# Contraction of the stacked attentions' score products: 96 rows before, 128 rows after, with 32 rows of zeros

## What is computed

```
q = _split_heads(x_q @ wq.T + bq)
k = _split_heads(x_kv @ wk.T + bk)
v = _split_heads(x_kv @ wv.T + bv)
scores = jnp.einsum('bhqd,bhkd->bhqk', q, k) * scale
attn = jax.nn.softmax(scores, axis=-1)
out = jnp.einsum('bhqk,bhkd->bhqd', attn, v)
return out @ wo.T + bo
...
x = x + _L1_xattn_ref(_layernorm(x, axis=-1), ctx_1024, ...)
x = x + _L1_ffn_ref(_layernorm(x, axis=-1), ...)
```

## Time and profile before

| | us |
|---|---|
| median of 3 runs | 4145.89 |
| lowest, highest | 4144.44, 4151.56 |
| the profiled execution, its own time | 4147.24 |
| span of the profiled execution, first to last instruction | 4145.4 |
| PE busy in the span | 3406.9 (82%) |
| DVE busy | 3363.0 (81%) |
| ACT busy | 2312.2 (56%) |
| POOL busy | 1555.2 (38%) |

### The profile page before, as it was taken

How to read it: one execution, slowest core, us unless ns; L and a number is a source line. 1 busy time by engine, 2 the same in 40 slices (tenths; PEclk the granted TensorE clock), 3 DMA queues, 4 the chain that set the end, 5 groups by cost and what they waited for, 6 DMA issues and landing times. The chain is left out here.

```text
span 4145.4 us, 95469 instructions
## 1 busy us (share of the span) xinstructions
PE 3406.9 (82%) x31830; PEld 2483.1 (60%) x31831; DVE 3363.0 (81%) x6145; ACT 2312.2 (56%) x4244; POOL 1555.2 (38%) x907
## 2 busy tenths in 40 slices
PE   6983979998599799994038839999499998899999
PEld 3553647776477477763026627777366666677777
DVE  7888879998799799996025569999788888788888
ACT  2431657776277466661025527777566665466665
POOL 1210035653000355542754435555155553122222
PEclk9985989999599899995569969999699998899999
DMA  1001222222000222211111242222222222000000
GB/s 64 14 27 68 124 52 64 67 63 54 36 0 0 53 63 63 63 40 46 52 53 59 63 123 67 61 64 61 60 58 51 52 57 75 26 16 15 13 12 15
DMA packets 158968, 208.77 MB, mean 50 GB/s; under 512 B 37820, under 2 KB 109824, under 8 KB 155585
## 3 DMA queue, kind: packets, MB, share of 16 engines
q1 hardware_dynamic: 149441, 187.83, 16.6%
q0 software_dynamic: 8192, 16.92, 1.2%
q10 hardware_dynamic: 1152, 1.57, 0.2%
HBM read 53.09 MB, written 42.21 MB: 23 GB/s over the span
## 5 line engine op out<-in xcount | busy, mean ns | idle before, releaser
L727 ACT ACTIVATE a_p<-a_p 128x480 f32<-128x480 f32 x832 | 503.2, 605 | 449.9 <-DVE a_p L572 442.8
L354 POOL TENSOR_TENSOR a_km<-a_k,a_slots 96x1920 fp32r<-96x1920 f32 x186 | 629.3, 3402 | 179.0 <-DMA a_k<-a_kh 179.0
L567 DVE TENSOR_REDUCE a_mx<-a_sc 128x4 f32<-128x480 f32 (+1 forms) x832 | 540.5, 650 | 67.2 <-PE a_sc L821 43.7
L572 DVE TENSOR_TENSOR a_p<-a_sc,a_mx 128x480 f32<-128x480 f32 x832 | 532.3, 640 | 19.1 <-issue 0.3
L733 ACT ACTIVATE a_pt<-a_tp 120x512 f32<-120x512 f32 x832 | 486.1, 585 | 77.0 <-PE a_tp L830 72.9
L830 PE MATMUL a_tp<-ident,a_p 128*120 128x128 f32 x3328 | 507.6, 275 | 4.1 <-ACT a_pt L733 4.1
L830 PEld LDWEIGHTS a_tp<-ident,a_p 128*120 128x120 f32 x3328 | 404.6, 138 | 80.0 <-issue 29.7
L815 PE MATMUL a_sc<-a_km,a_qr 96*128 96x480 f32 x768 | 396.9, 517 | 41.7 <-DVE a_p L572 24.6
L854 PE MATMUL a_nd<-a_pt,a_vm 120*32 120x128 f32 x6656 | 289.9, 281 | 9.4 <-ACT a_pt L733 9.0
L1806 ACT ACTIVATE f_s<-f_pu 128x512 f32<-128x512 f32 x256 | 153.7, 600 | 212.4 <-PE f_pv L1288 212.4
L854 PE MATMUL a_nd<-a_pt,a_dm 120*32 120x128 f32 x6656 | 263.7, 273 | 0.0
(11 more groups left out here) (431 smaller groups left out, 8853.2 us busy)
## 6 DMA issues: line engine op xcount, KB each, us to landing
a_qr<-a_qh SPq DMA_DIRECT2D x372, 64.0 KB, 2.0
a_k<-a_kh SPq DMA_DIRECT2D x384, 60.0 KB, 2.0
a_ctx<-in_ctxT SPq DMA_DIRECT2D x64, 240.0 KB, 2.7
a_qr<-a_ql SPq DMA_DIRECT2D x186, 64.0 KB, 2.0
a_k<-a_kl SPq DMA_DIRECT2D x192, 60.0 KB, 2.0
dispatched<-f_empty SPq DMA_DIRECT2D x8, 1040.0 KB, 21.0
f_xr<-dispatched SPq DMA_DIRECT2D x32, 260.0 KB, 2.6
chosen<-f_none SPq DMA_DIRECT2D x8, 1024.0 KB, 11.9
```

Of the source, the lines that this page charges most:

```text
L354: v.tensor_tensor(KM[par][:, i, :, :].rearrange("p b (j k) -> p b j k", k=KN), K3[:, i, :, :].unsqueeze(2).to_broadcast([TR, GB, 4, KN]), ...
L567: v.tensor_reduce(mx[:], view, AX.X, ALU.max).then_inc(mx_ready, 1)
L572: v.tensor_tensor(PR[s % 4][:].rearrange("p (h k) -> p h k", k=k), view, mx[:].unsqueeze(2).to_broadcast([P, heads, k]), ALU.subtract).the ...
L727: a.activation(PR[s % 4][:], PR[s % 4][:], ACT.Exp).then_inc(exp_ready, 1)
```

## The change

The tensors K3, QR and KM get 128 rows in place of 96, and `slots` too. Rows 96 to 127 are zeroed once per phase. The DMAs still fill rows 0 to 95. `masked_keys` now runs over 128 rows, so KM's last 32 rows become zero times zero, and L815 contracts over 128 rows; its number of columns stays. On DVE, four memsets per stacked phase are new: K3's, `slots`' and the first QR's rows behind `ln_group(0)`, the second QR's behind `masked_keys` of the opening. Two semaphores tell of them: POOL waits for the first before its first `masked_keys`, PE for the second before the first step and before every odd group.

```
-            K3 = sb(n_("k3"), [TR, 4, GB, KN])
-            QR = [sb(n_(f"qr{i}"), [TR, 4, GT], F32R) for i in range(2)]
+            K3 = sb(n_("k3"), [P, 4, GB, KN])
+            QR = [sb(n_(f"qr{i}"), [P, 4, GT], F32R) for i in range(2)]
...
-        slots = sb(n_("slots"), [TR, 4] if packed else [P, 4, STRIDE])
-        KM = [sb(n_(f"km{i}"), [TR, 4, GB, W], F32R) if packed else ...
+        slots = sb(n_("slots"), [P, 4] if packed else [P, 4, STRIDE])
+        KM = [sb(n_(f"km{i}"), [P, 4, GB, W], F32R) if packed else ...
...
                 low_part("k", 0)
+                pool.wait_ge(keys_empty, 2)
                 masked_keys(pool, nc.gpsimd, 0, 0, (0, 2))
...
                 ln_group(0)
+                if packed:
+                    v.memset(K3[TR:P], 0.0).then_inc(keys_empty, 1)
+                    v.memset(slots[TR:P], 0.0).then_inc(keys_empty, 1)
+                    v.memset(QR[0][TR:P].bitcast(F32), 0.0).then_inc(queries_empty, 1)
                 if bo is not None:
...
                 if packed:
                     dve.wait_ge(keys_first_in, 16 * n_first)
+                    dve.wait_ge(keys_empty, 2)
                     masked_keys(dve, v, 0, 0, (1, 3))
+                    v.memset(QR[1][TR:P].bitcast(F32), 0.0).then_inc(queries_empty, 1)
                 groups_loop(dve, group, 3 if U == 1 else 1)
...
                     if packed and j == 0:
+                        if i == 0 and par == 1:
+                            pe.wait_ge(queries_empty, 2)
                         pe.wait_ge(km_ready[i], g + 1)
...
+                if packed:
+                    pe.wait_ge(queries_empty, 1)
                 if own_keys:
                     groups_in_full(group)
```

More of the change, by code:

```diff
@@ L278, in attention_phase @@
             LOW = {"k": sb(n_("kl"), [P, GB * KN], F32R), "q": sb(n_("ql"), [P, GT], F32R)}
-            K3 = sb(n_("k3"), [TR, 4, GB, KN])
-            QR = [sb(n_(f"qr{i}"), [TR, 4, GT], F32R) for i in range(2)]
+            K3 = sb(n_("k3"), [P, 4, GB, KN])
+            QR = [sb(n_(f"qr{i}"), [P, 4, GT], F32R) for i in range(2)]
         CTX = [sb(n_(f"ctx{i}"), [P, GB, KN]) for i in range(2)] if not own_keys else None
-        slots = sb(n_("slots"), [TR, 4] if packed else [P, 4, STRIDE])
-        KM = [sb(n_(f"km{i}"), [TR, 4, GB, W], F32R) if packed else sb(n_(f"km{i}"), [P, GB, U, W]) for i in range(2)]
+        slots = sb(n_("slots"), [P, 4] if packed else [P, 4, STRIDE])
+        KM = [sb(n_(f"km{i}"), [P, 4, GB, W], F32R) if packed else sb(n_(f"km{i}"), [P, GB, U, W]) for i in range(2)]
         VW = D if hepos else NH * 32
@@ L316, in attention_phase @@
         prep_pool = sem(n_("prep_pool"))
+        keys_empty, queries_empty = sem(n_("keys_empty")), sem(n_("queries_empty"))
         f_psum = sem(n_("f_psum"))
@@ L354, in masked_keys @@
                 v.tensor_tensor(KM[par][:, i, :, :].rearrange("p b (j k) -> p b j k", k=KN),
-                                K3[:, i, :, :].unsqueeze(2).to_broadcast([TR, GB, 4, KN]),
-                                slots[:].unsqueeze(1).unsqueeze(3).to_broadcast([TR, GB, 4, KN]),
+                                K3[:, i, :, :].unsqueeze(2).to_broadcast([P, GB, 4, KN]),
+                                slots[:].unsqueeze(1).unsqueeze(3).to_broadcast([P, GB, 4, KN]),
                                 ALU.mult).then_inc(km_ready[i], 1)
@@ L374, in _ @@
                     sp.dma_start(cols[:, 1:2], bk.rearrange("(p a) -> p a", a=1)).then_inc(keys_first_in, 16)
-                sp.dma_start(slots[:], I["slots" if packed else "slot_classes"]).then_inc(keys_first_in, 16)
+                sp.dma_start(slots[0:TR] if packed else slots[:],
+                             I["slots" if packed else "slot_classes"]).then_inc(keys_first_in, 16)
                 if not own_keys:
```

## The result

The changed kernel takes 4170.49 us (median of 5 runs, 4164.72 to 4174.38); the kernel before, run beside it, 4146.57. The ratio is 1.0056, with a 95% interval of 1.0044 to 1.0068: some 23 us slower, where I had forecast 14 us and a range that ended at 4166. The profiled execution took 4165.07 us, with a span of 4163.3.

The account below looks back on a forecast made before the run. PE was taken to bound the steps, with DVE sharing in a1; added memsets lengthen the openings by 2 x 5.26 + 2 x 1.77 = 14.1 us, giving 4160 us (0.34% slower), range 4141 to 4166.

Parts of the forecast that it names:

- The 128-row products: Score products L815 in the steps: 128 rows instead of 96 cost and save nothing, zero for the 1024 products.
- Mask load: Weight load of mask product L821, late behind L815 in the steps: equal rows were taken to bring no gain.
- The rival: Unequal rows hold back L821's weight load, equal rows free it: 13 to 23 us gained, likeliest 4142 us; 24 in 100.
- The doubt that I gave: Against the mask-load rival: both late loads are also bf16 behind an fp32r product, which the trace cannot separate from unequal rows.
- My price of 17 to 30 ns a step: Mask-load rival's gain in each of 768 steps of a2, a3 and s3, from L821's 397 ns against L867's 380.
- POOL: Key masks over 128 rows cost nothing more; rival that POOL pays for rows, 1.13 us per mask, 4169 us: 7 in 100.
- Where the memsets cost: Openings: first three delay SP's bias DMAs in a1 and a2, are covered in a3 and s3; fourth delays every first maximum.
- What a memset costs: DVE memset: 0.833 ns an element plus 58 ns; K3 1.66 us, slots 0.06, each QR 1.77.
- DMAs do as before: Rest of the kernel: SP, ACT and the DMAs were taken to behave as before, adding no time.
- the cover of 3.99 us: s3's opening: free time between bias DMAs and first DMA into K3, said to cover the three memsets' 3.60 us.
- The signs to look for: L821's load and mean unchanged; a1 and a2 bias DMAs 3.5 us later, first maximum 5.3; a3 and s3 1.8; POOL 3.4 us.

Follow-up runs that it names:

- the two runs that split the change: Changed kernel with its memsets on GpSimd, 128 rows kept: 4150.86 us, ratio 1.0013; changed kernel with memsets on VectorE, products and key masks over 96 rows: 4167.74 us, 1.0062.
- the turned order: Kernel before, 96 rows, with the mask's bf16 product issued ahead of the scores' product in a2, a3 and s3: 4135.98 us, ratio 0.9973.
- the half-size run: Changed kernel with products and key masks over 96 rows and the three large memsets over half their size: 4155.8 us, one execution.
- the version that went the other way: Kernel before, 96 rows, no memsets, with SP's bias transfers moved behind the keys' twelve: 4143.41 us, ratio 0.9994.

## Why the prediction was right and wrong

**The 128-row products** cost and gain nothing: right, by the stages above and by the two runs that split the change.

**Mask load.** The rival was false. Rows aren't why it is late; with equal rows it is as late as before. The doubt that I gave, that it is a bf16 load behind an fp32r product, fits the turned order, in which the fp32r load behind the bf16 product is in time. But the type alone doesn't decide: a stretch of the kernel before, in f0, has a bf16 load of 96 columns (L1516) behind an fp32r product, both of 128 rows, and it comes 3 ns after that product's start (time line, PE and its weight loads):

```profile
416.94 0.40 PE L1288 MATMUL f_po<-f_al,f_downhi 128*128 128x512 f32 x1
...
416.95 0.47 PEld L1516 LDWEIGHTS f_pt<-ident_bf,f_gs 128*96 128x96 bf16 x4
```

What makes the mask's load late stays open. My price of 17 to 30 ns a step was too narrow: turning the order saved 10.72 us / 256 = 42 ns a step in a2 and 26 in a3; the 8 in s3 are no more than its steps vary between executions, though its pair of products became as much shorter as theirs.

**POOL** doesn't pay for rows: right, 3407 against 3402 ns, and 8.64 us for either count.

**Where the memsets cost** was right: ahead of SP's bias transfers in a1 and a2, ahead of the first maximum in all four, next to nothing (0.07 us) for the three in a3.

**What a memset costs is the step that failed.** I took the duration of the earlier trace rows for the price, though the time line of the kernel before showed what it leaves out:

```profile
1113.05 1.34 DVE L1408 MEMSET f_g<- 128x1536 uint32 x1 [0.27 <-issue]
```

0.27 us of waiting for nothing stand ahead of it, and 0.27 + 1.34 = 1.61 is the price. The Trainium skill's page VectorE: DVE Perf Modes (Zero memsets can be issued as uint32), weighed in the prediction, gives 1.60 for it as an estimate, at one cycle an element and 0.96 GHz, and I let the row stand against the page. The page was right: the half-size run shows 1.05 ns an element. Another page of the Trainium skill, PSUM — Partial Sum Buffer (Specifications (TRN2)), gives 1.04 ns an element on trn2 for VectorE's memset of 2-byte elements into PSUM, "timed from the profile rows around it"; no run here writes PSUM so, but the 1.05 into SBUF is the same price, and it had to be read off the rows around in the same way.

The fourth memset's price has a second part: the first maximum used to start 0.07 us ahead of the key masks' end, and no longer does. Two terms were missing. Pushed back by 4.38 us, the keys' transfers met ACT's query transfers: 1.45 and 0.89 us. I had written that DMAs do as before. And in s3 the cover of 3.99 us, enough for 3.60, isn't enough for the 4.5 that the three take there. The sum, mended:

| term | forecast, us | measured, us |
|---|---|---|
| three memsets, a1 and a2 | 2 x 3.49 | 2 x 4.38 |
| fourth memset, four phases | 4 x 1.77 | 4 x 2.35 |
| later landing of the keys, a1 and a2 | 0 | 1.45 + 0.89 |
| first key mask later in s3 | 0 | 0.54 |
| DVE's normalising later in a1 | 0 | 0.3 |
| sum | 14.1 | 21.3 |
| the four openings | | 21.4 |

With the memsets alone at their true price, 8.8 + 9.4 = 18.2 us, the forecast would have been 4164; the two missing terms take it to 4167, just past the end of the range. The 0.3 us in a1 stand where DVE waited for the output bias 6.90 us instead of 6.60. The last 3 us up to the median are no larger than f2 alone varies from execution to execution, and I give them no cause. **The signs to look for** held, with other sizes: SP's bias transfers of a1 moved from 563.18 - 549.50 = 13.68 us behind the phase's first operation to 568.40 - 550.04 = 18.36, 4.7 later where I said 3.5.

## What to carry to other kernels

Price an instruction by the distance between the starts of its neighbours, not by its row alone: idle time that ends with "issue" belongs to it if it grows with its size. A short operation costs most where an engine that issues transfers in order waits for it, so before adding one ask which queue stands behind, and what the pushed transfer or operation will meet there: here keys met queries, and in the version that went the other way POOL's masks met DVE's normalising. When a change turns out to be neutral in one part (here the rows), the order of two operations in the same line can still be worth more than all of it.

## What the hardware showed that I had not expected

- A DVE memset's row reads 0.83 ns an element, while with the idle time ahead of it the memset grows by 1.05; the difference stands as idle time ahead of it (0.16 us at 1024 elements, 0.38 at 2048).
- The same keys' transfers land in 3.3 us with ACT's six query transfers held back and in 4.7 us beside them, in a1.
- Two key masks on POOL stretch four normalising instructions of DVE from 1.11 to 7.17 us.
- In a pair of accumulating products, the bf16 load behind the fp32r product came 0.33 us after that product's start, with 96 rows as with 128, and the fp32r load behind the bf16 product 10 ns after the other load; the order is worth 42 ns a step in a2.
